# Causal attention in one core: softmax sums taken by ScalarE's exponentials instead of by a column of ones in V

## What is computed

```python
q = (x @ wq.T + bq).reshape(B, S, H, hd)      # k and v in the same way
scores = jnp.einsum('bqhd,bkhd->bhqk', q, k) * inv_sqrt_hd
scores = jnp.where(causal[None, None, :, :], -jnp.inf, scores)
probs = jax.nn.softmax(scores, axis=-1)
attn = jnp.einsum('bhqk,bkhd->bqhd', probs, v).reshape(B, S, D)
x = x + layernorm(attn @ wo.T + bo)
```

## Time and profile before

| | |
|---|---|
| median of 3 runs | 2382.2 us |
| the profiled execution | 2380.48 us |
| its span | 2378.7 us |
| mean granted TensorE clock | 0.987 |
| busy: TensorE, VectorE, ScalarE, POOL | 2269.8, 1712.3, 1732.0, 1645.7 us |

### The profile page before, as it was taken

One profiled execution on the slowest core, in us unless ns is written; L12 is line 12 of the kernel. 1 busy time (PEld: TensorE's weight loads), 2 busy tenths in 40 slices (PEclk: granted clock), 3 DMA queues, 4 the chain that ended last, 5 costly groups with the idle time before them and its releaser, 6 DMA issues. The chain is left out here.

```text
span 2378.7 us, 70852 instructions
## 1 busy us (share of the span) xinstructions
PE 2269.8 (95%) x28738; PEld 1451.0 (61%) x28738; DVE 1712.3 (72%) x4174; ACT 1732.0 (73%) x2369; POOL 1645.7 (69%) x1282
## 2 busy tenths in 40 slices
PE   8999999999999998899999999999999779999996
PEld 5566767575757665557575757575766545545453
DVE  8577777777777766567777777777676737777777
ACT  6587777877788766677777777777787745666665
POOL 3588888888888876678888888888898622222221
PEclk9999999999999999999999999999999989999998
DMA  7799999999999999999999999999999976666662
GB/s 214 142 194 197 198 211 205 209 194 212 213 201 205 199 199 200 201 205 195 198 196 212 192 197 195 204 195 203 185 199 185 211 174 155 170 151 169 152 167 80
DMA packets 1365237, 451.10 MB, mean 190 GB/s; under 512 B 1306641, under 2 KB 1339809, under 8 KB 1364913
## 3 DMA queue, kind: packets, MB, share of 16 engines
q1 hardware_dynamic: 1364912, 446.58, 100.7%
HBM read 72.14 MB, written 46.14 MB: 50 GB/s over the span
## 5 line engine op out<-in xcount | busy, mean ns | idle before, releaser
L1134 POOL TENSOR_TENSOR hl<-probs,hl 128x1024 f16<-128x1024 f32 x539 | 1163.2, 2165 | 178.5 <-ACT hl L987 176.1
L977 ACT ACTIVATE probs<-s_ps,exp_bias 128x1024 f32<-128x1024 f32 (+7 forms) x768 | 633.0, 853 | 258.8 <-DVE exp_bias L793 248.4
L788 DVE TENSOR_REDUCE neg_max<-s_ps 128x1 f32<-128x1024 f32 (+7 forms) x768 | 676.2, 904 | 146.7 <-PE s_ps L564 143.9
L987 ACT ACTIVATE hl<-probs 128x1024 f16<-128x1024 f32 x539 | 569.7, 1057 | 121.4 <-DMA pt<-hl 75.5
L590 PE MATMUL o_ps<-v,pt 128*128 128x65 f16 x4352 | 429.8, 193 | 23.9 <-DMA pt<-hl 18.8
L591 PE MATMUL o_ps<-v,pt 128*128 128x65 f16 x4352 | 430.1, 194 | 0.0
L590 PEld LDWEIGHTS o_ps<-v,pt 128*128 128x128 f16 x4352 | 400.3, 96 | 47.9 <-DMA pt<-hl 15.4
L592 PE MATMUL o_ps<-v,pt 128*128 128x65 f16 x4352 | 428.9, 192 | 0.0
L564 PE MATMUL s_ps<-nat 64*128 64x512 f16 (+3 forms) x3840 | 405.4, 349 | 23.2 <-ACT probs L977 20.3
L591 PEld LDWEIGHTS o_ps<-v,pt 128*128 128x128 f16 x4352 | 399.5, 97 | 19.3
L592 PEld LDWEIGHTS o_ps<-v,pt 128*128 128x128 f16 x4352 | 399.9, 98 | 0.0
(11 more groups left out here) (183 smaller groups left out, 3639.0 us busy)
## 6 DMA issues: line engine op xcount, KB each, us to landing
w_raw<-in_w_pairs SPq DMA_DIRECT2D x46, 576.0 KB, 5.1
o_scratch<-o_hl SPq DMA_DIRECT2D x64, 256.0 KB, 3.0
out<-result SPq DMA_DIRECT2D x31, 512.0 KB, 3.4
x_in<-in_x SPq DMA_DIRECT2D x27, 512.0 KB, 4.9
pt<-hl SPq DMA_TRANSPOSE x539, 5.5
xn_scratch<-xn SPq DMA_DIRECT2D x16, 512.0 KB, 4.5
xn<-in_x SPq DMA_DIRECT2D x11, 512.0 KB, 4.1
x_in_c<-in_x SPq DMA_DIRECT2D x10, 512.0 KB, 4.2
```

The lines of the kernel that those rows point to most:

```text
L788: nc.vector.tensor_reduce(neg_max[:, step.round, acc, h:h + 1], s_ps[(n + h) % S_RING][:, first:end], AX_X, ALU.max, negate=True).then_inc ...
L977: last = nc.scalar.activation(probs_of(n)[:, cols], s_ps[n % S_RING][:, cols], ACT.Exp, bias=exp_bias[:, step.round, acc, h:h + 1], scale= ...
L987: nc.scalar.activation(hl_of(n, 0), probs_of(n), ACT.Copy).then_inc(p_hi_done, 1)
L1134: nc.gpsimd.tensor_tensor(hl_of(n, 1), probs_of(n), hl_of(n, 0), ALU.subtract).then_inc(p_lo_done, 1)
```

## The change

The column of ones goes: V's memsets at the start of VectorE's program, the 65th column of each output product, and the wait of TensorE for the memsets. Each exponential of ScalarE also writes the sum of what it made (`accum_out`) into `prob_sum`. In the step that closes a round, VectorE makes from these sums, in five small instructions (`output_gain`), the reciprocal of the short row's sum and, for the long row, `gain` = factor / sum. `output_read` then multiplies with `gain`, so that `output_sum` is one reduction that writes finished rows, and POOL's `long_rows` is gone. ScalarE's `chunk_factors` waits for `gain_done` of the round before instead of `part_done`. The exponential's semaphore now comes after the accumulator has been read.

```diff
--- before.py
+++ after.py
@@ -224,8 +224,11 @@
         exp_bias = sb("exp_bias", [P, N_ROUND, 3, 2], F32)
         bias_min = sb("bias_min", [P, 2], F32)
         factor = sb("factor", [P, 2, 2], F32)
-        o_part = sb("o_part", [P, 2, 2, HD + 1], F32)
-        o_long = sb("o_long", [P, 2, HD + 1], F32)
+        o_part = sb("o_part", [P, 2, 2, HD], F32)
+        prob_sum = sb("prob_sum", [P, N_ROUND, 3, 2], F32)
+        part_sum = sb("part_sum", [P, 2, 2], F32)
+        long_sum = sb("long_sum", [P, 2], F32)
+        gain = sb("gain", [P, 2, 2], F32)
         inv_long = sb("inv_long", [P, 2], F32)
         inv_short = sb("inv_short", [P, 2], F32)
 
@@ -246,12 +249,10 @@
         minus_half = sb("minus_half_a", [P, 1], F32)
 
         s_ps, o_ps, u_ps = fin["s_ps"], fin["o_ps"], fin["u_ps"]
-        o_acc = o_ps[:, 0:6 * (HD + 1)].rearrange("p (a h f) -> p a h f", a=3, h=2)
+        o_acc = o_ps[:, 0:6 * HD].rearrange("p (a h f) -> p a h f", a=3, h=2)
 
...
@@ -583,7 +586,7 @@
                 blocks = [(k0 + k, acc) for t, k0, nb, acc in step.parts for k in range(nb)]
                 for at, (k, acc) in enumerate(blocks):
                     hi, lo = pt_of(n)[:, at, :], pt_of(n)[:, step.blocks + at, :]
-                    v_hi, v_lo = (v[p % 2][:, k, part, h, 0:HD + 1] for part in range(2))
+                    v_hi, v_lo = (v[p % 2][:, k, part, h, 0:HD] for part in range(2))
                     dst = o_acc[:, acc, h, :]
                     first = step.opens and h == 0 and at == 0
                     last = step.closes and h == 1 and at == step.blocks - 1
@@ -685,7 +688,6 @@
             project(0, 2, KT // 2, KT)
             for u in range(3, LAST_CHUNK):
                 project(0, u, 0, ATOMS[order_of(0)[u][0]])
-            pe.wait_ge(set_done, 2)
             pe.wait_ge(full_done, LAST_CHUNK)
             for i in range(LAG):
                 scores(0, i)
@@ -700,12 +702,6 @@
 
         @block.vector
         def _(dve):
-            for i in range(2):
-                nc.vector.memset(v[i][:].rearrange("p t l h f -> p (t l h f)"), 0.0).then_inc(zeros_set, 1)
-            dve.wait_ge(zeros_set, 2)
-            for i in range(2):
-                nc.vector.memset(v[i][:, :, 0, :, HD:HD + 1], 1.0).then_inc(set_done, 1)
-
             def norm_stats(i, tile, loaded, n):
                 dve.wait_ge(loaded, 16 * (n + 1))
                 for h in range(2):
@@ -802,31 +798,45 @@
                 nc.vector.tensor_reduce(bias_min[:], exp_bias[:, r, 0:2, :].rearrange("p c h -> p h c"), AX_X,
                                         ALU.min).then_inc(min_done, 1)
 
+            def output_gain(p, r):
+                n = N_ROUND * p + r
+                dve.wait_ge(exp_done, NTASK * p + 2 * first_step(p, r + 1))
+                dve.wait_ge(factor_done, n + 1)
+                if n >= 1:
+                    dve.wait_ge(gain_done, n)
+                    dve.wait_ge(part_done, n)
+                    dve.wait_ge(short_done, n)
+                nc.vector.tensor_tensor(part_sum[:], prob_sum[:, r, 0:2, :], factor[:], ALU.mult).then_inc(part_sum_done, 1)
+                nc.vector.reciprocal(inv_short[:], prob_sum[:, r, 2, :]).then_inc(inv_short_done, 1)
+                dve.wait_ge(part_sum_done, n + 1)
+                nc.vector.tensor_reduce(long_sum[:], part_sum[:].rearrange("p c h -> p h c"), AX_X, ALU.add).then_inc(
+                    long_sum_done, 1)
+                dve.wait_ge(long_sum_done, n + 1)
+                nc.vector.reciprocal(inv_long[:], long_sum[:]).then_inc(inv_long_done, 1)
+                dve.wait_ge(inv_long_done, n + 1)
+                nc.vector.tensor_tensor(gain[:], factor[:], inv_long[:].unsqueeze(1).broadcast_to([P, 2, 2]),
+                                        ALU.mult).then_inc(gain_done, 1)
+
             def output_read(p, r):
                 n = N_ROUND * p + r
                 dve.wait_ge(pv_done, NTASK * p + 2 * first_step(p, r + 1))
-                dve.wait_ge(factor_done, n + 1)
+                dve.wait_ge(gain_done, n + 1)
+                dve.wait_ge(inv_short_done, n + 1)
                 if n >= 1:
-                    dve.wait_ge(sum_done, n)
-                nc.vector.tensor_tensor(o_part[:], o_acc[:, 0:2], factor[:].unsqueeze(3).broadcast_to([P, 2, 2, HD + 1]),
+                    dve.wait_ge(long_done, n)
+                nc.vector.tensor_tensor(o_part[:], o_acc[:, 0:2], gain[:].unsqueeze(3).broadcast_to([P, 2, 2, HD]),
                                         ALU.mult).then_inc(part_done, 1)
-                nc.vector.reciprocal(inv_short[:], o_acc[:, 2, :, HD]).then_inc(inv_short_done, 1)
-                dve.wait_ge(inv_short_done, n + 1)
                 if n >= 4:
                     dve.wait_ge(o_lo_done, n // 4)
-                nc.vector.tensor_tensor(o_rows[:, 1, slot_of(rounds_of(p)[r][1]) % 4], o_acc[:, 2, :, 0:HD],
+                nc.vector.tensor_tensor(o_rows[:, 1, slot_of(rounds_of(p)[r][1]) % 4], o_acc[:, 2],
                                         inv_short[:].unsqueeze(2).broadcast_to([P, 2, HD]), ALU.mult).then_inc(
                     short_done, 1)
 
             def output_sum(p, r):
                 n = N_ROUND * p + r
                 dve.wait_ge(part_done, n + 1)
-                if n >= 1:
-                    dve.wait_ge(long_done, n)
-                nc.vector.tensor_reduce(o_long[:], o_part[:].rearrange("p c h f -> p h f c"), AX_X, ALU.add).then_inc(
-                    sum_done, 1)
-                dve.wait_ge(sum_done, n + 1)
-                nc.vector.reciprocal(inv_long[:], o_long[:, :, HD]).then_inc(inv_long_done, 1)
+                nc.vector.tensor_reduce(o_rows[:, 0, slot_of(rounds_of(p)[r][0]) % 4],
+                                        o_part[:].rearrange("p c h f -> p h f c"), AX_X, ALU.add).then_inc(long_done, 1)
 
             def turned_low(n, half):
                 dve.wait_ge(turned_hi_done, turned_count(n, half) + 1)
@@ -882,6 +892,8 @@
                         row_max(*step)
                     if evacuate:
                         output_sum(*done)
+                    if steps_of(p)[i].closes:
+                        output_gain(p, r)
                     split = next_split(p, i - 1)
                     if split:
                         split_weight(*split)
@@ -975,7 +987,8 @@
                 for t, k0, nb, acc in step.parts:
                     cols = slice(at, at + nb * P)
                     last = nc.scalar.activation(probs_of(n)[:, cols], s_ps[n % S_RING][:, cols], ACT.Exp,
-                                                bias=exp_bias[:, step.round, acc, h:h + 1], scale=SOFTMAX_SCALE)
+                                                bias=exp_bias[:, step.round, acc, h:h + 1], scale=SOFTMAX_SCALE,
+                                                accum_out=prob_sum[:, step.round, acc, h:h + 1])
                     at += nb * P
                 last.then_inc(exp_done, 1)
                 for old in HL_BEFORE[n]:
@@ -995,7 +1008,7 @@
                 n = N_ROUND * p + r
                 act.wait_ge(min_done, n + 1)
                 if n >= 1:
-                    act.wait_ge(part_done, n)
+                    act.wait_ge(gain_done, n)
                 for h in range(2):
                     last = nc.scalar.activation(factor[:, :, h], exp_bias[:, r, 0:2, h], ACT.Exp,
                                                 bias=bias_min[:, h:h + 1], scale=-1.0)
@@ -1139,15 +1152,6 @@
                 nc.gpsimd.tensor_tensor(dst_of(p, m, c, 1), shaped(m, full[u % 2]), dst_of(p, m, c, 0),
                                         ALU.subtract).then_inc(unit_lo_done, 1)
 
-            def long_rows(p, r):
-                n = N_ROUND * p + r
-                pool.wait_ge(inv_long_done, n + 1)
-                if n >= 4:
-                    pool.wait_ge(o_lo_done, n // 4)
-                nc.gpsimd.tensor_tensor(o_rows[:, 0, slot_of(rounds_of(p)[r][0]) % 4], o_long[:, :, 0:HD],
-                                        inv_long[:].unsqueeze(2).broadcast_to([P, 2, HD]), ALU.mult).then_inc(
-                    long_done, 1)
-
             def rows_low(n):
 
                 pool.wait_ge(o_hi_done, n + 1)
@@ -1158,8 +1162,6 @@
             def body(p, kind):
                 for i in range(NSTEP):
                     step = step_of(p, i, kind)
-                    if steps_of(p)[i].opens and (p or i):
-                        long_rows(*((p, steps_of(p)[i].round - 1) if i else (p - 1, N_ROUND - 1)))
                     if step:
                         probs_low(*step, 0)
                     if i == half_done(p) or i == 0 and p > 0:
@@ -1174,7 +1176,6 @@
                     for tile in norm_tiles(p, i, 0):
                         norm_scale(LN_TILES + tile)
                 if kind == "last":
-                    long_rows(p, N_ROUND - 1)
                     rows_low(2 * p + 1)
 
             norm_scale(0)
```

6 lines of the change are left out of this document (3 added, 3 removed).

## The result

The change makes the kernel slower: 2410.1 us (median of 4 runs, 2407.2 to 2414.9) against 2383.5 us for the kernel before, measured beside it (2379.8 to 2385.2). The ratio is 1.0115, 95% interval [1.0099, 1.0131], so 24 to 31 us. The forecast was 2372 us in a range of 2364 to 2385: wrong in sign and outside its range. The profiled execution took 2410.1 us; its span is 2408.3, which is 29.6 more than the profiled span before. Its mean granted clock was 0.985 (0.987 before). Executions of the kernel before at 0.985 took 2379 to 2388 us, and both long full stretches were granted 1.00 before and after, so the clock doesn't explain the difference.

What follows compares the result with a forecast made beforehand. TensorE was taken to bound the kernel in two long full stretches, the other engines having room. Terms -10.6 + 2.2 + 0 - 2 - 0.3 = -10.7 us gave 2369.8 or 2371.5, shaded to 2372 us, range 2364 to 2385.

Steps and rivals of the forecast that it cites:

- The step that failed: VectorE: five small instructions in, two reciprocals out, net +0.3 us by 128 rounds; booked 0, at most +6.6 us.
- no exponential waits for them at once: VectorE's closing step: the five instructions stand behind the maxima of scores 3 steps ahead, so booked at 0.
- Products: TensorE's output products, 65 to 64 columns: 1.0 ns less each for 10608 products, -10.6 us (ends 0 and -13.1).
- rivals A and B: Output products: A, only one column's 4.4 us gained, 2378 us; B, weight loads keep 30.2 ns, 2382 us; chance 0.2 each.
- the odd column count: Output products: 65 columns cost extra for being odd; at 64 the pace falls onto the line, 1.0 ns less.
- Reads: ScalarE's accumulator reads behind 768 exponentials: 22 waits of TensorE grow by 0.1 us each, +2.2 us (0.7 to 12).
- Rival C: ScalarE's reads release TensorE late: some 20 to 28 us more waits, up to 2395, 2389 in the middle; chance 0.1.
- C's two signs: High half 1.4 us or more behind its exponential; over 35 us of waits of scores for ScalarE.
- C's own sum: ScalarE's late release, 20 to 28 us against a product gain of 10.6 or less: up to 2395, 2389 in the middle.
- POOL: 128 long rows and their waits go, so low halves and transposes come earlier: -2 us (ends 0 and -8).
- Start: V's memsets leave VectorE's start, so the first norm begins up to a microsecond earlier: -0.3 us (ends 0 and -1.2).

Runs made afterwards that it cites:

- x4_five_alone: Kernel before, with five instructions of the same kinds and shapes added at each round's close, results unused; 2411.3 us, ratio 1.0130.
- z3_no_gain: The change without `output_gain`; `gain` and `inv_short` are constants, so rows are not divided by their sums; 2376.9 us, ratio 0.9977.
- y1_one_element: The change with all products of `output_gain` as TENSOR_SCALAR of one element a partition, ten small instructions instead of five; 2401.6 us, ratio 1.0074.
- y2_v_packed: y1_one_element with V's tile at 64 columns a head instead of 66; 2398.6 us, ratio 1.0064.
- z1_gain_early: y2_v_packed with `output_gain` moved to the end of the step before the closing one; 2384.7 us, ratio 1.0023.
- x3_columns_alone: Kernel before, output products with 64 of 65 columns, outputs still 65 apart in PSUM, division by the sum left out; 2378.4 us, ratio 0.9985.
- y4_no_long_rows: Kernel before without POOL's long rows and the reciprocal ahead of them, rows not divided by their sums, V 1024 times smaller; 2379.2 us, ratio 0.9989.

## Why the prediction was wrong

**The step that failed** is VectorE's: "The closing step gains five small dependent instructions of about 0.15 to 0.2 us, some 0.7 us", booked at 0, with 6.6 us as the upper end. It measured about 30 us: +30 alone (x4_five_alone), -33 when taken out (z3_no_gain). Two things were wrong in it. The durations came from the earlier trace rows, where the small instructions were reciprocals and a reduction, and none had two inputs in SBUF. The nearest in kind beside a busy POOL were large: of the 46 splits of the kernel before, 41 take 1.22 us and five 1.7 to 2.5, each of which ends 1.36 us behind the end of a POOL instruction. The wait was there to be read. In place of 0.15 to 0.2 us came waits of up to 2.1 us for the POOL instruction that was running, and POOL stood at 85%. The second error is the overlap: the 25% of idle time on VectorE was taken as room anywhere, and "no exponential waits for them at once" stopped at the scores already done. The group reaches the next ones: it pushes what stands ahead of `output_read` (at one place the `xn` row, which then meets POOL itself), and with it the maxima behind, which start 0.78 us after their scores in the mean instead of 0.20, and it holds up the projected units (17 us of TensorE's waits).

How the 33 us divide, from the runs: forms that don't wait at the same place 8.5 to 10 us (change to y1_one_element), the place 10 to 14 us (y2_v_packed to z1_gain_early), V's packing 2 to 3 us (y1_one_element to y2_v_packed, a gain of TensorE and no part of this price), and z1_gain_early is 8 to 11 us above z3_no_gain, though with packed V. So at least that much stays with ten short instructions at their best place tried. Waits and place are not additive: the same move costs 44 us with one form (up to 15 of it the clock) and gains 10 to 14 with the other. How much five instructions that neither wait nor are ten would cost was not separated.

The parts measured alone, +10 for the reads, -3 for the columns, +30 for the group and -3 for POOL, make +34 us. With the pace that x3_columns_alone didn't reach, worth some 4 us more, that is +30 against a measured +27, which is agreement within their intervals.

**Products** (-10.6): the pace came nearly as forecast, 0.86 ns each by 1.381 against 1.421 us, which is 9.1 us for the 10608, and rivals A and B fall. The reading behind it, the odd column count, holds for head 0, which goes from 30.2 to 29.1 ns with 64 columns alone. For head 1 it doesn't: 30.3 stays 30.4 until the outputs are packed in PSUM (29.6) and V in SBUF (29.2 in y2_v_packed). That the change packs the outputs as well is luck for the forecast. The rule quoted in it, from the Trainium skill's "TensorE: Matmul & The Clock Gate", Back-to-back issue gap, gives 29.2 ns at 64 columns, and y2_v_packed shows 29.1 to 29.2. How much of the 9 us becomes time in the change was not measured by itself; where the pace was measured with the time (x3_columns_alone, 5 us by the pace and 1 to 6 in time; y2_v_packed, 3 and 2 to 3), the two agree.

**Reads** (+2.2): mis-sized. The step from an exponential's start to its high half grew by 0.09 us in a task of one part (medians 1.19 and 1.28), not by 0.03. The estimate took the 0.12 us from an activation's end to its dependent successor in the earlier trace rows; behind an exponential out of PSUM it is 0.18. Why it is more there isn't shown. The step between two exponentials of a task grew by 0.09 too, as forecast. The price in time is 10 to 13.5 us, at the upper end of 12 that the text gave. Rival C asked for 0.4 us to decide; a quarter of it was enough for half of its price, and the slower side came mainly from VectorE. One of C's two signs came up for this reason, over 35 us of waits of scores for ScalarE (40.3), and the other, a high half 1.4 us behind its exponential, did not. (C's own sum, 20 to 28 us against -10.6, -2 and -0.3, gives 2389 to 2397, so 2389 was its low end and not its middle.)

**POOL** (-2): fits y4_no_long_rows (-2.6, interval -5.5 to +0.2), but can't be told from nothing, and nor can **Start** (-0.3).

Without the failed step the forecast's sum was -10.7 us; z3_no_gain, which is the change without that step, measured -5.5 (-8.8 to -2.1) by its ratio. With the reads at their measured price, 8 to 11 us more, the sum would be -3 to 0, which meets the upper part of that interval; whether the terms overlap can't be said from it.

## What to carry to other kernels

Before a small instruction goes onto VectorE beside a busy GpSimd, look at its form as well as its size: here 4 elements a partition with two SBUF inputs cost up to 2.1 us, and one element as TENSOR_SCALAR 0.2 to 0.3. Idle time of an engine is room only at the place where it idles: look at what stands next in its order, and at what that will meet when it starts a microsecond later. No version tried here with all sums computed beat the kernel before: the best, z1_gain_early, is 0.1 to 0.3% slower.

## What the runs showed of the hardware

- TENSOR_TENSOR of 128x4 and TENSOR_SCALAR of 128x2 on VectorE waited for the large POOL instruction that was running (149 of 256 and 153 of 256 over 0.3 us); TENSOR_SCALAR of 128x1, RECIPROCAL of 128x2 and TENSOR_REDUCE to 128x2 did not (0.15 to 0.27 us). Beside a POOL instruction of 128x1, `gain` didn't wait either (five cases, 0.16 us).
- Whichever of the two begins first holds up the other: a weights' split that begins 0.36 us ahead of POOL's low half takes 1.21 us and the low half 2.84 instead of 2.13; one that begins behind it takes up to 2.86.
- Output products of 64 columns start 29.1 to 29.2 ns apart with V packed. With head 1's V at byte 132 they are 29.6 in head 1, and with its output at an odd column of PSUM as well 30.4. Those of 65 columns take 30.2 and 30.3.
- An accumulator read takes 0.19 us behind an exponential out of PSUM and puts 0.09 us between the exponential and what follows, be it dependent (0.09 to 0.18 us behind its end) or not (0.10 to 0.01 us ahead of it).
